# Decoder layer: the gate and up products of the first FFN unit in two halves of 256 tokens

## Chip, cores and metric

One core of a Trainium2 chip runs the whole program. The metric is device microseconds for one execution, lower is better.

## The reference

A decoder layer over 4 sequences of 512 tokens and width 512, in float32, with three stages; each ends in a layer norm (the first and second called x1 and x2 here). Cut to what matters:

```python
x1 = layernorm(x + attention(x))               # K and V with rotation, A = sum over tokens of cos(K) * cos(V)
q  = fp8(x1 * 448 / max|x1|);  c = fp8(ctx * 448 / max|ctx|)     # one scale for the whole tensor
x2 = layernorm(x1 + x1 + (q @ c) * unscale + mask)
mlp = silu(x2 @ gate_w) * (x2 @ up_w) @ down_w                   # 512 -> 2048 -> 512
out = layernorm(x2 + x2_mlp_and_experts)       # plus 8 of 1024 experts per token, chosen by two key tables
```

## The kernel before

The program is written by hand for five engines: each has its own queue, which runs in order, and waits for counts of semaphores. Tokens lie in tiles of 128 (16 tiles; four make a sequence), and the four sequences are called 0 to 3. All large matrices are multiplied in float32r with each operand split into a high part and the rest (w_hi, w_lo, x2_hi, x2_lo), so a product of the FFN is three: hi*hi, lo*hi, hi*lo. One product has 128x128 stationary values and 512 moving columns, the tokens of a sequence. The FFN weights are cut into 8 groups of 256 columns; a unit is one group for one sequence, so there are 32 units, 0 to 3 for group 0. In a unit, gate_up (L1918) makes for each of two blocks of 128 columns (c = 0 and 1) a gate product into bank gu[2c] and an up product into gu[2c+1], 12 matrix products each; down (L1951) or down_early (L1969) multiplies the result with the down weights into the four banks ob.

The change lies where the first program block (attention, x1) ends and the second begins, at 210 us, and in unit 0. What happens there before:

- The largest |x1| of all tokens is only known at the block's end, so the rounding of x1 to fp8 can start only now. For each tile ScalarE scales (L1439) and takes a rounded magnitude (L1441), both in `scaled`; VectorE adds and subtracts it (L1580, L1582, here called raise and lower), in `quantise`. TensorE multiplies with the rounded context in `cross` (L1915). The x1 of the later sequences comes to ScalarE by TensorE's transposes (L1907), through banks gu.
- VectorE adds the product to x1 (L1605, `first_residual`) and gives the negative mean (L1607). ScalarE squares the difference and sums it (L1454, `deviation`). VectorE gives the variance for two tiles (L1612), GpSimd takes the power -1/2 (L1327, `power_pair`), VectorE normalises (L1616). Then TensorE transposes x2 (L1898), ScalarE copies it as x2_hi (L1447), VectorE subtracts for x2_lo (L1627). All of this is done for the four tiles, step by step: all four rounded, then all four residuals, and so on.
- While TensorE has nothing to do, `keep_running` (L2015) lets it transpose the identity.
- The first gate products (L1933) wait for x2_hi of all four tiles, then those with x2_lo (L1936) for all four of x2_lo; the up products follow (L1888 to L1890), then `cross` of sequence 1, transposes of x1 of sequence 2, the products of c = 1 and down_early.
- The weights of group 0's down matrix are loaded at the start of the second block into w_stage[0]; ScalarE makes their high part behind x2_hi, VectorE their low part behind the first product silu(gate)*up.
- GpSimd issues the DMA that adds the mask to x1 of a sequence (L149, `add_mask`) once its x1 is transposed; at the start of the block that of sequence 1 stands ahead of both powers, later add_mask(n+2) ahead of power(n+1).
- Behind unit 0 sequence 1 has its own residuals, normalisation and transposes, which sequence 1's unit needs.

## Time and profile before

| | |
|---|---|
| median of 3 runs | 790.26 us (789.82 to 790.3) |
| the profiled execution, its own time | 789.89 us |
| span of its instructions | 788.1 us |
| TensorE busy | 770.3 us (98%) |
| VectorE busy | 665.8 us (84%) |
| ScalarE busy | 321.5 us (41%) |
| GpSimd busy | 369.1 us (47%) |

The profile names TensorE's products PE and its loads of stationary values PEld, VectorE DVE, ScalarE ACT, GpSimd POOL. Products overlap: each is shown with a duration of 0.39 us, but the next starts 0.23 us behind it, so rates are read from starts. A duration is one execution's. Idle time in brackets stands before an instruction with the engine that ended it.

### The profile page before, as it was taken

What the parts mean: (1) busy time and instruction counts of PE and PEld (TensorE: products, weight loads), DVE (VectorE), ACT (ScalarE), POOL (GpSimd) and SP (SyncE); (2) the same over time, 40 slices, a digit from 0 to 9 for tenths busy, and PEclk for the clock granted to TensorE, in tenths of its full rate; (3) what the DMA queues carried; (4) which work ended last, traced back from release to release, by engine and by line L of the source; (5) the groups of instructions that cost most, each with busy time, mean ns of one, the idle gap of its engine ahead of it and who ended that gap; (6) DMA issues with size and microseconds to landing.
All of it is one profiled execution on the core that took longest, in us unless ns stands there. A gap on an engine that the chain in (4) does not pass through costs nothing.

```text
span 788.1 us, 10623 instructions
## 1 busy us (share of the span) xinstructions
PE 770.3 (98%) x3550; PEld 631.3 (80%) x3550; DVE 665.8 (84%) x1351; ACT 321.5 (41%) x700; POOL 369.1 (47%) x323
## 2 busy tenths in 40 slices
PE   8999998999899999999999999999999999999997
PEld 6888887878667778888888888888888888888885
DVE  6889789998898870476789998999999999899876
ACT  6454346455574422222443433334333343344324
POOL 1242331432122411014466676776776677676324
PEclk9999999999999999999999999999999999999999
DMA  8666513715465638001122221431333223242014
GB/s 323 241 129 166 93 55 85 190 21 86 73 146 117 150 89 286 1 0 33 61 70 78 82 88 41 128 95 47 90 110 111 90 79 115 62 128 61 17 54 160
DMA packets 51190, 79.78 MB, mean 101 GB/s; under 512 B 17503, under 2 KB 26335, under 8 KB 50624
## 3 DMA queue, kind: packets, MB, share of 16 engines
q0 software_dynamic: 24240, 31.52, 19.0%
q1 hardware_dynamic: 25312, 47.59, 17.2%
q8 instruction: 28, 0.46, 0.2%
q10 hardware_dynamic: 1584, 0.01, 0.1%
q14 instruction: 26, 0.21, 0.1%
HBM read 110.50 MB, written 12.58 MB: 156 GB/s over the span
## 4 chain that ended last, share of the span: by engine, by line
PE 64%; DVE 4%; issue 2%; POOL 2%; ACT 1%; POOLq 0%; ACTq 0%; DVEq 0%
PE gu L1888 14%; PE gu L1889 14%; PE gu L1890 14%; PE ob L1962 7%; PE ob L1961 7%; PE ob L1966 7%; DVE scratch L1580 1%; DVE scratch L1582 1%; POOL h_lo L1316 1%; DVE x_lo L1627 1%; PE gu L2060 0%; PE ob L1915 0%; ACT junk L1454 0%; DVE xall L1621 0%; PE ob L1982 0%
## 5 line engine op out<-in xcount | busy, mean ns | idle before, releaser
L1888 PE MATMUL gu<-x_hi,w_hi 128*128 128x512 f32 x516 | 201.4, 390 | 0.0
L1890 PE MATMUL gu<-x_hi,w_lo 128*128 128x512 f32 x516 | 200.8, 389 | 0.0
L1889 PE MATMUL gu<-x_lo,w_hi 128*128 128x512 f32 x516 | 200.8, 389 | 0.0
L1316 POOL TENSOR_TENSOR h_lo<-mid,h_hi 128x512 fp32r<-128x512 f32 x62 | 87.0, 1421 | 175.8 <-ACT h_hi L1466 175.8
L1890 PEld LDWEIGHTS gu<-x_hi,w_lo 128*128 128x128 f32 x516 | 96.9, 188 | 20.2
L1888 PEld LDWEIGHTS gu<-x_hi,w_hi 128*128 128x128 f32 x516 | 96.9, 188 | 20.0
L1889 PEld LDWEIGHTS gu<-x_lo,w_hi 128*128 128x128 f32 x516 | 96.9, 188 | 19.9
L1476 ACT ACTIVATE gates<-dots 128x1 f32<-128x1 f32 x144 | 29.1, 202 | 175.2 <-DVE dots L1729 175.2
L1638 DVE TENSOR_TENSOR mid<-gu,mid 128x512 f32<-128x512 f32 x64 | 43.9, 686 | 64.1 <-PE gu L1890 54.2
L1961 PE MATMUL ob<-w_hi,h_hi 128*128 128x512 f32 x224 | 87.1, 389 | 0.0
L1962 PE MATMUL ob<-w_lo,h_hi 128*128 128x512 f32 x224 | 87.1, 389 | 0.0
L1335 POOL DMA_INDIRECT ctx_q<-table_dram,row_i x64 | 73.5, 1149 | 18.8 <-issue 17.0
L1335 POOL DMA_INDIRECT scratch<-table_dram,row_i x64 | 73.0, 1141 | 16.5 <-issue 15.1
L1466 ACT ACTIVATE h_hi<-mid 128x512 fp32r<-128x512 f32 x62 | 36.2, 625 | 85.3 <-PE ob L1966 62.2
L1966 PE MATMUL ob<-w_hi,h_lo 128*128 128x512 f32 x224 | 68.9, 389 | 0.0
L1460 ACT ACTIVATE mid<-gu 128x512 f32<-128x512 f32 x64 | 37.8, 590 | 58.9 <-PE gu L1890 50.3
L1801 DVE TENSOR_TENSOR xall<-ob,xall 128x512 f32<-128x512 f32 x93 | 58.7, 683 | 3.6 <-PE ob L1966 1.6
L1311 POOL TENSOR_TENSOR w_lo<-xhat,w_hi 128x1024 fp32r<-128x1024 f32 x21 | 50.4, 2400 | 24.1 <-ACT w_hi L1430 15.9
L1729 DVE CUSTOM_DVE_ANT_0 junk<-x_tok,ctx_q 128x512 bf16<-128x512 f32 x64 | 60.4, 944 | 0.5
L1738 DVE SCALAR_TENSOR_TENSOR xall<-ctx_q,coef,xall 128x512 f32<-128x512 f32 x64 | 60.1, 939 | 0.0
L1738 DVE SCALAR_TENSOR_TENSOR xall<-scratch,coef,xall 128x512 f32<-128x512 f32 x64 | 59.5, 930 | 0.0
L1729 DVE CUSTOM_DVE_ANT_0 junk<-x_tok,scratch 128x512 bf16<-128x512 f32 x64 | 57.1, 892 | 0.3
(254 smaller groups left out, 1431.9 us busy)
## 6 DMA issues: line engine op xcount, KB each, us to landing
stage<-in_ctx SPq DMA_DIRECT2D x7, 1024.0 KB, 6.8
total<-prod POOLq DMA_DIRECT2D x11, 384.0 KB, 4.1
xall<-half_bo POOLq DMA_DIRECT2D x4, 1024.0 KB, 9.6
xhat<-in_L_ffn_gate_w SPq DMA_DIRECT2D x8, 512.0 KB, 3.4
xhat<-in_L_ffn_up_w SPq DMA_DIRECT2D x8, 512.0 KB, 3.4
xall<-in_mask_Bx1xS_ff POOLq DMA_DIRECT2D x4, 1024.0 KB, 11.0
xhat<-in_L_ffn_down_w SPq DMA_DIRECT2D x8, 512.0 KB, 3.6
x_dram<-xall SPq DMA_DIRECT2D x4, 1024.0 KB, 7.0
```

Source lines behind the costliest of these rows:

```text
L1311: nc.gpsimd.tensor_tensor(flat(lo, r), stage_of(r, slot), flat(hi, r).bitcast(F32), ALU.subtract).then_inc(wlo_done, 1)
L1316: nc.gpsimd.tensor_tensor(lo[:, c], mid[c][:], hi[:, c].bitcast(F32), ALU.subtract).then_inc(hlo_done, 1)
L1335: nc.gpsimd.indirect_dma_start(rows[k], None, table_dram[:, :], bass.IndirectOffsetOnAxis(ap=row_i[t % 2][:, k:k + 1], axis=0), bounds_che ...
L1729: nc.vector.tensor_tensor_reduce(out=junk2[:], in0=x2_tok[par][:], in1=row[:, 0:D], scale=1.0, scalar=0.0, op0=ALU.mult, op1=ALU.add, accu ...
L1738: nc.vector.scalar_tensor_tensor(tile(t), row[:, D:2 * D], coef[:, t % 2, k:k + 1], tile(t), ALU.mult, ALU.add).then_inc(pick_done, 1)
L1801: nc.vector.tensor_tensor(tile(j), ob[i][:], tile(j), ALU.add).then_inc(acc_done, 1)
L1888: nc.tensor.matmul(dst, lhs[0], rhs[0], start=start, stop=False)
L1889: nc.tensor.matmul(dst, lhs[0], rhs[1], start=False, stop=False)
L1890: return nc.tensor.matmul(dst, lhs[1], rhs[0], start=False, stop=stop)
L1961: nc.tensor.matmul(ob[i][:], h[0][:, c, ts], w_high[:, c], start=(c == 0), stop=False)
L1962: nc.tensor.matmul(ob[i][:], h[0][:, c, ts], w_low[:, c], start=False, stop=False)
L1966: last = nc.tensor.matmul(ob[i][:], h[1][:, c, ts], w_high[:, c], start=False, stop=(c == GC - 1))
```

## The change

On TensorE, the gate and up products of unit 0 are cut in halves of 256 tokens (tiles 0 and 1, tiles 2 and 3) by two new functions, each for one bank. `high_half` makes the 8 products with x2_hi (both parts of the weights), `low_half` the 4 with x2_lo. The other products of x1 and x2 are put in between.

```diff
+                def high_half(half, c, r):
+                    pe.wait_ge(wlo_done, r + 1)
+                    pe.wait_ge(h2_done, TB // 2 * (half + 1))
+                    if half == 0:
+                        pe.wait_ge(y_scaled, TB + 2 * c + r + 1)
+                    w, cols, fs = (gate_s, up_s)[r][0], half_cols(half), slice(c * P, (c + 1) * P)
+                    for k in range(KC):
+                        for h in range(2):
+                            nc.tensor.matmul(gu[2 * c + r][:, cols], w[h][:, k, fs], x2_hi[:, k, cols], start=(half == 0 and k == 0 and h == 0), stop=False, skip_group_check=True)
+
+                def low_half(half, c, r):
+                    pe.wait_ge(l2_done, TB // 2 * (half + 1))
...
+                    for k in range(KC):
+                        last = nc.tensor.matmul(gu[2 * c + r][:, cols], w[0][:, k, fs], x2_lo[:, k, cols], start=False, stop=(half == 1 and k == KC - 1), skip_group_check=True)
+                    if half:
+                        last.then_inc((gate_mm, up_mm)[r], 1)
...
-                for i in range(TB):
+                for i in range(2):
                     transposes(1, (i,), own_bank, x1t_mm, freed(y_done, 0))
                     cross(0, nothing, (i,))
-                pe.wait_ge(y_done, TB + 2)
-                for i in range(1, TB):
+                transposes(1, (2, 3), own_bank, x1t_mm, freed(y_done, 0))
+                for i in range(2):
                     pe.wait_ge(minus_first, i + 1)
-                    keep_running(gu[0], 7)
-                pe.wait_ge(v3_ready, 2)
-                keep_running(gu[0], 4)
-                x2_transposes(0, nothing)
-                keep_running(gu[0], 3)
-                for n in range(TB - 1):
-                    gate_up(n, 0, n, 0, 2 if n == 0 else None)
-                    cross(n + 1, freed(acc_done, TB * (n - 1)) if n else nothing)
+                    keep_running(ob[3], 6)
+                cross(0, nothing, (2,))
+                x2_transposes(0, nothing, (0, 1))
+                cross(0, nothing, (3,))
+                for r in range(2):
+                    high_half(0, 0, r)
+                for r in range(2):
+                    low_half(0, 0, r)
+                high_half(0, 1, 0)
+                x2_transposes(0, nothing, (2, 3))
+                high_half(0, 1, 1)
+                for r in range(2):
+                    low_half(0, 1, r)
+                for r in range(2):
+                    high_half(1, 0, r)
+                for r in range(2):
+                    low_half(1, 0, r)
+                cross(1, nothing)
+                transposes(2, (0, 1), x1_bank(2), x1t_mm, first_half_free(0))
+                high_half(1, 1, 0)
+                low_half(1, 1, 0)
+                transposes(2, (2, 3), x1_bank(2), x1t_mm, freed(y_done, TB * 2 - 2))
+                high_half(1, 1, 1)
+                low_half(1, 1, 1)
+                down_early(0, 0, freed(z2_done, 0))
```

TensorE, from the transposes of x1 of the last tile (before) or the last two (after) to the first gate product (L2015 and L2065 are fillers, L1907 and L1939 transposes of x1 of sequence 1, L1915 and L1947 cross products of sequence 0, L1898 and L1930 transposes of x2). Before:

```order
L1907 MATMUL gu<-ident,xall 128x128 x4
L1915 MATMUL ob<-ctx_q,scratch 128x512 x4
L2015 MATMUL gu<-ident 128x128 x25
L1898 MATMUL ob<-ident,xall 128x128 x16
L2015 MATMUL gu<-ident 128x128 x3
L1933 MATMUL gu<-x_hi,w_hi 128x512
```

After:

```order
L1939 MATMUL gu<-ident,xall 128x128 x8
L2065 MATMUL ob<-ident 128x128 x12
L1947 MATMUL ob<-ctx_q,scratch 128x512 x4
L1930 MATMUL ob<-ident,xall 128x128 x8
L1947 MATMUL ob<-ctx_q,scratch 128x512 x4
L1991 MATMUL gu<-x_hi,w_hi 128x256
```

The first product of gate now follows the transposes of two tiles of x2 and the cross product of tile 3; the other two tiles are transposed further on, between products.

On VectorE, rounding, residuals, normalisation and x2_lo are cut in the same way, and the low part of the down weights (w_lo<-xhat) moves to the front. Before, at the end of the rounding (the first row is the lower of tile 2, the next two raise and lower tile 3):

```order
L1582 SCALAR_TENSOR_TENSOR scratch<-x_tok,scratch 128x512
L1580 SCALAR_TENSOR_TENSOR scratch<-x_tok,scratch 128x512
L1582 SCALAR_TENSOR_TENSOR scratch<-x_tok,scratch 128x512
L1605 SCALAR_TENSOR_TENSOR xall,z_sum<-ob,unscale,xall 128x512
L1607 TENSOR_SCALAR z_minus<-z_sum 128x1
```

After, from the second block's first row:

```order
L1655 TENSOR_TENSOR w_lo<-xhat,w_hi 128x2x512
L1597 SCALAR_TENSOR_TENSOR scratch<-scratch 128x512
L1601 SCALAR_TENSOR_TENSOR scratch<-scratch 128x512
L1597 SCALAR_TENSOR_TENSOR scratch<-scratch 128x512
L1601 SCALAR_TENSOR_TENSOR scratch<-scratch 128x512
L1775 TENSOR_TENSOR unscale<-scale_x,scale_c 128x1
L1777 TENSOR_SCALAR unscale<-unscale 128x1
L1628 SCALAR_TENSOR_TENSOR xall,z_sum<-ob,unscale,xall 128x512
L1630 TENSOR_SCALAR z_minus<-z_sum 128x1
```

The first residual (L1628, before L1605) now stands behind the rounding of two tiles, not of four. Its rest, from VectorE's part of the diff:

```diff
+                first_low_w(2, 2, 0)
+                quantise(0, (0, 1))
...
-                quantise(0, range(TB))
-                for i in range(TB):
-                    first_residual(i)
+                first_residual(0)
+                first_residual(1)
+                quantise(0, (2,))
                 first_variance(0)
+                raised = raise_y(0, 3)
+                first_normalise(0)
+                first_normalise(1)
+                lower_y(3, raised)
+                first_residual(2)
+                first_residual(3)
+                low_x2(0, (0, 1))
                 first_variance(1)
-                for i in range(TB):
-                    first_normalise(i)
-                low_x2(0)
-                quantise(1, range(TB))
+                quantise(1, (0,))
+                first_normalise(2)
+                first_normalise(3)
+                quantise(1, (1,))
+                low_x2(0, (2, 3))
+                quantise(1, (2, 3))
                 for n in range(TB - 1):
                     middle(n, 0)
-                    if n == 0:
-                        first_low_w(2, 2, 0)
```

ScalarE follows the same order, and the down weights are loaded and their high part is made in the first block already, behind the centring of the first tile of sequence 3:

```diff
+                sp.wait_ge(wlo_done, 1)
+                sp.dma_start(w_stage[0].rearrange("p (c n) -> p c n", c=GC), down_v[:, 0]).then_inc(w_in_s[0], 16)
...
                 for i in range(TB - 1):
                     centre_x1(LAST, i)
                     if i:
                         scale_x1(LAST, i - 1)
+                    else:
+                        high_down()
...
                 scaled(0, range(TB))
-                scaled(1, (0, 1))
-                for i in range(TB):
-                    deviation(i)
+                deviation(0)
+                deviation(1)
+                for i in range(3):
+                    scale_y(1, i)
+                magnitude(1, 0)
+                high_x2(0, (0, 1))
+                deviation(2)
+                deviation(3)
+                scale_y(1, 3)
+                for i in range(1, TB):
+                    magnitude(1, i)
+                high_x2(0, (2, 3))
```

GpSimd, from the second block's start (rstd is the power, L149 the DMA that adds a mask, h_lo the low part of the unit's result). Before:

```order
L1344 MEMSET key_sb 128x256
L149 DMA xall<-in_mask_Bx1xS_ff 128x4x512
L1327 TENSOR_TENSOR rstd<-var,neg_half 128x2 x2
L1316 TENSOR_TENSOR h_lo<-mid,h_hi 128x512
L149 DMA xall<-in_mask_Bx1xS_ff 128x4x512
L1322 TENSOR_TENSOR rstd<-var,neg_half 128x4
```

After:

```order
L1352 MEMSET key_sb 128x256
L1335 TENSOR_TENSOR rstd<-var,neg_half 128x2
L149 DMA xall<-in_mask_Bx1xS_ff 128x4x512
L1335 TENSOR_TENSOR rstd<-var,neg_half 128x2
L1324 TENSOR_TENSOR h_lo<-mid,h_hi 128x512
L1330 TENSOR_TENSOR rstd<-var,neg_half 128x4
L149 DMA xall<-in_mask_Bx1xS_ff 128x4x512
```

The mask of a sequence now goes out behind the power of the one before it.

## Rows read from the trace of the kernel before

**Rows 1.** List of cores: core, span, mean granted clock of TensorE.

```profile
core 0: 788.1 us, clock 0.999
```

**Rows 2.** What TensorE waited for, 225 to 788 us: total, times, longest.

```profile
PE gu L1933 <- issue: 0.4, 1, 0.4
```

**Rows 3.** Timeline of TensorE: start, us, engine, line, operation, count.

```profile
213.10 1.04 PE L1915 MATMUL ob<-ctx_q,scratch 128*128 128x512 bf16 x4 [0.86 <-DVE scratch L1582]
213.97 0.60 PE L1907 MATMUL gu<-ident,xall 128*128 128x128 f32 x4
214.43 1.04 PE L1915 MATMUL ob<-ctx_q,scratch 128*128 128x512 bf16 x4
...
222.20 2.21 PE L1898 MATMUL ob<-ident,xall 128*128 128x128 f32 x16
...
225.18 0.47 PE L1933 MATMUL gu<-x_hi,w_hi 128*128 128x512 f32 x1 [0.44 <-issue]
...
228.03 0.39 PE L1888 MATMUL gu<-x_hi,w_hi 128*128 128x512 f32 x1
...
230.75 3.63 PE L1915 MATMUL ob<-ctx_q,scratch 128*128 128x512 bf16 x16
...
241.47 0.39 PE L1978 MATMUL ob<-w_hi,h_hi 128*128 128x512 f32 x1
```

**Rows 4.** Timeline of ScalarE, same columns; idle time before it in brackets.

```profile
201.03 0.72 ACT L506 ACTIVATE xall<-xall,minus_m 128x512 f32<-128x512 f32 x1 [1.01 <-POOL minus_m L363]
...
211.43 0.67 ACT L1439 ACTIVATE scratch<-gu,scale_x 128x512 f32<-128x512 f32 x1
...
212.67 0.67 ACT L1439 ACTIVATE scratch<-gu,scale_x 128x512 f32<-128x512 f32 x1
...
214.61 0.63 ACT L1441 ACTIVATE x_tok<-scratch 128x512 bf16<-128x512 f32 x1
...
217.92 0.72 ACT L1454 ACTIVATE junk<-xall,z_minus 128x512 bf16<-128x512 f32 x1 [0.20 <-DVE z_minus L1607]
...
222.85 2.23 ACT L1447 ACTIVATE x_hi<-ob 128x512 fp32r<-128x512 f32 x4 [1.40 <-PE ob L1898]
```

**Rows 5.** Timeline of VectorE, same columns.

```profile
193.52 2.35 DVE L742 TENSOR_TENSOR w_lo<-xhat,w_hi 128x1024 fp32r<-128x1024 f32 x2
...
211.63 0.69 DVE L1580 SCALAR_TENSOR_TENSOR scratch<-scratch 128x512 f32<-128x512 bf16 x1 [1.08 <-ACT scratch L1441]
212.35 0.69 DVE L1582 SCALAR_TENSOR_TENSOR scratch<-scratch 128x512 bf16<-128x512 bf16 x1
212.96 0.68 DVE L1580 SCALAR_TENSOR_TENSOR scratch<-scratch 128x512 f32<-128x512 bf16 x1
...
216.94 0.74 DVE L1605 SCALAR_TENSOR_TENSOR xall<-ob,unscale,xall 128x512 f32<-128x512 f32 x1
...
217.82 0.75 DVE L1605 SCALAR_TENSOR_TENSOR xall<-ob,unscale,xall 128x512 f32<-128x512 f32 x1
...
221.49 0.17 DVE L1612 TENSOR_SCALAR var<-z_square 128x2 f32<-128x2 f32 x1 [0.90 <-ACT junk L1454]
221.56 2.14 DVE L1616 TENSOR_SCALAR xall<-xall,z_minus,rstd 128x512 f32<-128x512 f32 x4
223.62 2.48 DVE L1627 TENSOR_TENSOR x_lo<-ob,x_hi 128x512 fp32r<-128x512 f32 x4
```

**Rows 6.** Timeline of GpSimd, same columns.

```profile
221.74 0.93 POOL L1327 TENSOR_TENSOR rstd<-var,neg_half 128x2 f32<-128x2 f32 x1 [0.33 <-DVE var L1612]
```

**Rows 7.** Routing products (L2060): duration min/median/max, first and last start.

```profile
L2060 PEld LDWEIGHTS gu<-key_sb,ctx_q x32: 187/192/192, 315.9 to 319.5; 128*128 128x128 f32 x32
L2060 PE MATMUL gu<-key_sb,ctx_q x32: 270/275/276, 316.2 to 319.6; 128*128 128x128 f32 x32
```

**Rows 8.** Busy time of each engine, 217.95 to 222.20 us, with TensorE's clock.

```profile
217.95:222.20 4.25, 3.29 (x26) 2.70 (x26) 3.25 (x13) 3.23 (x8) 2.11 (x3) 1.00 0.66 99
```

**Rows 9.** Page, part 6: DMA issues, KB each, us to landing.

```profile
x_dram<-xall SPq DMA_DIRECT2D x4, 1024.0 KB, 7.0
```

More of the change, by code:

```diff
@@ L1235, in _ @@
                         sp.dma_start(key_sb[half * DQ:(half + 1) * DQ, s, half], keys[s]).then_inc(key_in, 16)
-                load(2, 0, 2)
                 load(3, 0, 3)
@@ L1349, in _ @@
                     low_h(n, 0)
+                    if n + 1 < TB:
+                        power(n + 1)
                     if n + 2 < TB:
                         add_mask(n + 2)
-                    if n + 1 < TB:
-                        power(n + 1)
                     low_h(n, 1)
@@ L1430, in high_w, with scale_y, magnitude, high_x2 @@
                     nc.scalar.activation(flat(hi, r), stage_of(r, slot), ACT.Copy).then_inc(whi_done, 1)
+                def scale_y(b, i):
+                    j = TB * b + i
+                    act.wait_ge(x1t_mm, j + 1)
+                    if j >= TB:
+                        act.wait_ge(q_done, j - TB + 1)
+                    nc.scalar.activation(y_q[i], gu[x1t_bank(b, i)][:], ACT.Copy, scale=scale_x[:, 0:1]).then_inc(y_scaled, 1)
+                def magnitude(b, i):
+                    act.wait_ge(y_scaled, TB * b + i + 1)
+                    nc.scalar.activation(m_q[i], y_q[i], ACT.Abs, scale=ROUND_TO_4_BITS).then_inc(y_done, 1)
                 def scaled(b, tiles):
                     for i in tiles:
-                        j = TB * b + i
-                        act.wait_ge(x1t_mm, j + 1)
-                        if j >= TB:
-                            act.wait_ge(q_done, j - TB + 1)
-                        nc.scalar.activation(y_q[i], gu[x1t_bank(b, i)][:], ACT.Copy, scale=scale_x[:, 0:1]).then_inc(y_scaled, 1)
-                        act.wait_ge(y_scaled, j + 1)
-                        nc.scalar.activation(m_q[i], y_q[i], ACT.Abs, scale=ROUND_TO_4_BITS).then_inc(y_done, 1)
-                def high_x2(b):
-                    for i in range(TB):
+                        scale_y(b, i)
+                        magnitude(b, i)
+                def high_x2(b, tiles=range(TB)):
+                    for i in tiles:
                         j = TB * b + i
@@ L1570, in _, with raise_y, lower_y @@
                 own.base, own.n = 0, first_steps[0]
+                def raise_y(b, i):
+                    dve.wait_ge(y_done, TB * b + i + 1)
+                    if b and i == 0:
+                        dve.wait_ge(cross_mm, TB * b)
+                    return own.did(nc.vector.scalar_tensor_tensor(y_q[i], m_q[i], ROUND_SUBNORMAL, y_q[i], ALU.max, ALU.add))
+                def lower_y(i, raised):
+                    own.wait(raised)
+                    nc.vector.scalar_tensor_tensor(x_q[:, i].rearrange("p c n -> p (c n)"), m_q[i], ROUND_SUBNORMAL, y_q[i], ALU.max, ALU.subtract).then_inc(q_done, 1)
                 def quantise(b, tiles):
                     for i in tiles:
[L1574 to L1582 removed]
+                        lower_y(i, raise_y(b, i))
                 def residual(b, tiles):
@@ L1621, in normalise, with low_x2 @@
                         nc.vector.tensor_scalar(tile(TB * b + i), tile(TB * b + i), mv2[:, i, 0:1], rstd2[:, i:i + 1], ALU.subtract, ALU.mult).then_inc(x2_done, 1)
-                def low_x2(b):
-                    for i in range(TB):
+                def low_x2(b, tiles=range(TB)):
+                    for i in tiles:
                         j = TB * b + i
@@ L1890, in three, with x2_transposes @@
                     return nc.tensor.matmul(dst, lhs[1], rhs[0], start=False, stop=stop)
-                def x2_transposes(b, free):
-                    for i in range(TB):
+                def x2_transposes(b, free, tiles=range(TB)):
+                    for i in tiles:
                         free(i)
```

36 lines of the change are left out of this document (17 added, 19 removed).

## The prediction

> **What bounds the kernel now.** I read four views in this order. The list of cores gives the span and the clock: 788.1 us at a granted clock of 0.999 [rows 1], the higher level (2.4 GHz) throughout. The list of what TensorE waited for, from 225 us to the end, has one line: 0.4 us before the first gate product of FFN unit 0 [rows 2]. So from 225.18 us on TensorE sets the time, and whatever moves its stream there moves the end. The same holds behind unit 2: nothing there runs by a clock of its own (the stores of x2, the table copy and the routing all start from TensorE's or VectorE's results), and it shifts as a whole.
>
> The timelines of the four engines show the stretch before that, 210 to 225 us. There TensorE does only 16 transposes of x1, 16 products of the cross attention, 16 transposes of x2 and filler transposes [rows 3]. The end of the stretch is set by a chain over all four tiles in turn: ScalarE scales x1, VectorE rounds (raise, lower), TensorE multiplies, VectorE adds the residual, ScalarE squares, GpSimd takes the power, VectorE normalises, TensorE transposes, ScalarE copies x2_hi [rows 3 to 6]. The change shortens the chain to the first product by asking for two tiles instead of four. It pays on TensorE with twice as many products of half the width.
>
> **Start of the first product.** Steps read off the rows: a raise is followed by its lower 0.72 us later and that by the next raise 0.61 later, 1.33 a tile [rows 5]. The two raises and lowers of tiles 0 and 1 start at 211.63 as before and leave VectorE free at 214.29. The low part of the down weights now stands ahead of them (two such parts took 2.35, so 1.2 [rows 5]); VectorE waits for the first magnitude until 211.63 [rows 5], so it costs 0, and without that idle time 1.2. The two small operations on unscale, 0.17 each like the variance [rows 5], come next, about 0.36 with their wait. Residual 0 starts at 214.65 instead of 216.94; its product has been ready since 214.14 (213.10 plus 1.04 [rows 3]). Residual 1 follows 0.88 later (216.94 to 217.82) at 215.53, the raise and lower of tile 2 at 216.41 and 217.13, the variance at 217.74. The two squares begin 0.98 behind their residual (217.92 against 216.94 [rows 4, 5]) at 215.63 and take 0.89 each (four between 217.92 and 221.49), so they are ready at 217.41. From a variance to the normalisation that needs it are 0.25 to GpSimd's start and 0.93 of power [rows 5, 6], 1.20 in all: 218.94. GpSimd is free for it because the power now stands ahead of the mask. The normalisations start 0.53 apart (four in 2.14), the lower of tile 3 follows at 220.00, and its product 0.75 behind (212.35 to 213.10 [rows 3, 5]) at 220.75. The transposes of tiles 0 and 1 start 0.64 behind their normalisation (221.56 to 222.20) and are over by 220.6. The product of tile 3 holds TensorE 0.87 us (213.10 to 213.97 [rows 3]), and x2_hi of both tiles is ready before that ends (0.65 behind the transposes, 222.20 to 222.85 [rows 3, 4]). **First gate product: 221.62 instead of 225.18, minus 3.56 us.**
>
> **What is given back.** (a) The products with x2_lo wait for VectorE: residual 3 needs the last cross product (220.75 plus 1.04, some 221.87), 0.88 later come two low parts at 0.61 each (four in 2.48 [rows 5]), ready at 224.05. TensorE has 16 half-width products until then, to 223.54: **plus 0.51**. (b) The transposes of tiles 2 and 3 used to lie ahead of the stream and are now in it. Four transposes take 0.46 (213.97 to 214.43 [rows 3]), two tiles 0.92, with the change of kind taken as **1.0**. They don't wait: the second variance goes out at 223.97, the power comes back at 225.17, VectorE is in a raise and lower until 225.37, the transposes can go at 226.0, and TensorE gets there at 224.05 plus 16 products, 225.97. (c) The width, 96 half products for 48 whole ones. A whole one takes 0.2267 (12 between 228.03 and 230.75 [rows 3]), 10.88 in all. The trace has no product of 256 columns. Below, half of 0.2267 is 0.1133, since the same columns must pass. Above, the routing products have 128 columns with the same size of weights and start every 0.110 (31 intervals between 316.2 and 319.6 [rows 7]), and the straight line from 128 columns at 0.110 to 512 at 0.2267 gives 0.149 at 256. I take 0.12, near the lower end: the 0.110 at a quarter of the columns looks like a floor that the load of the weights sets, the columns need 0.1133, and if the two overlap as they do at 512 the larger counts, with a little for two limits that meet. 96 times 0.12 is 11.52, **plus 0.64**. (d) A new wait: the transposes of x1 of sequence 2 into banks 0 and 1 need the magnitudes of their first two tiles. Behind the first transpose ScalarE needs 0.65 to start, 1.24 for a tile (211.43 to 212.67), 0.70 and 0.63 for the second's scale and magnitude (214.61 is 0.70 behind 211.43 plus two tiles [rows 4]), 3.22. TensorE used to fill this with 12 whole products; it now has 12 halves (1.44) and three times 0.46, 2.82: **plus 0.40**. Behind it on TensorE stands everything else.
>
> **Edits at nothing.** The high part of the down weights moves to ScalarE at 200.0, where it sat idle for 1.01 us ahead of 201.03 [rows 4]; the operation is as long as that gap. Its data is asked for when the first low part is done, about 194.7 [rows 5], beside a mask transfer. 1024 KB by the same queue landed in 7.0 [rows 9], so 512 KB should land before 201; later, it would push the last maxima of x1 one for one. GpSimd's mask for sequence 1 goes out behind the first power, at some 219.9; what needs it, the first residual of sequence 1, comes behind a product that starts at 231.8 (rival B), so it has 13 us, where a store of the same 1024 KB took 7.0 [rows 9]. The store of x2 of sequence 0 goes out with the last normalisation of that sequence, some 3 us later, and its first reader stands behind the first down products, beyond 240. Filler transposes stand only where TensorE waits.
>
> **The sum** is minus 3.56 plus 0.51, 1.0, 0.64 and 0.40: **minus 1.0 us**. The profiled execution took 789.89 (1.8 outside the span), which gives 788.9; the median of the runs is 790.26, 0.37 above it, and I carry that over: 789.3.
>
> **A rule of the skill.** The routing rows say that a load of 128 columns of weights can start every 0.110 us and hides beside a product [rows 7]. The Trainium skill (TensorE: Matmul & The Clock Gate, LDWEIGHTS) gives the load 128/1.2, 107 ns, however few columns are multiplied, and its section Back-to-back issue gap gives N/2.4 + 2.5, 109 ns at 256 columns. By these two the halves would cost 96 times 0.109 and the change would bring 1.7 us instead of 1.0. The same formula gives 216 ns for 512 columns where the rows show 227, so I don't follow it to the end.
>
> **The rivals.** **A, the narrow product is dear.** At 0.149 the 96 products cost 2.8 more than at 0.12; 0.46 of it falls into wait (a) and 0.35 into wait (d), 2.0 remain, and the change is 1.0 slower than before: 791.2. It decides at 0.135. For it speaks that the load of weights, which 512 columns hid, has no room left; against it that loads of 187 to 192 ns each still start every 0.110, so they overlap [rows 7]. **B, the next chain takes the gain.** The cross products of sequence 1 now start at 221.62 + 0.51 + 1.0 + 72 x 0.12 = 231.8, 1.0 later than before (230.75), because half 0 of both column blocks stands ahead of them. What follows, residuals to x2 of sequence 1 and the products of h on TensorE, is then no earlier. Against it: VectorE no longer has the 1.2 us of down weights in that chain and GpSimd's power no longer stands behind the mask. If it still binds, about 0.2 is left: 790.1. **C, the clock falls.** TensorE's busy share in the emptiest part, 217.95 to 222.20, is 3.29 of 4.25 at clock 1.00 [rows 8]; between 217.5 and 221.6 it would be 2.66 of 4.1. If the chip granted 1.2 GHz there, each of the half products after it would take twice as long: 48 of them cost 5.8, 795. No row shows the clock falling in a comparable gap. **D, the columns alone count.** At 0.109 to 0.113 a product, with waits as worked out, the change brings 1.4 to 1.7: 788.6. **E, the change doesn't do what it says:** the first product starts no earlier because the masks or the power of the first pair are late. The order of GpSimd's work excludes it as far as the rows go; I count it with B.
>
> **How the numbers follow.** Forecast 0.54, A 0.18, B and E 0.14, D 0.07, C or a product above 0.16 us 0.07. The likeliest is 789.3. A measurement of this kernel tells apart about 0.2%, 1.6 us. Faster than that is below 788.7: D and the lower part of the forecast (both waits gone, 0.9 more), 0.07 plus 0.11. Slower is above 791.8: C with its neighbours, and the upper part of A, 0.07 plus 0.08. Within: 0.67. The range 788.4 to 791.6 takes in D and A with 0.4 for the medians.
>
> **What would show it.** In the profile after: the first product of 256 columns at 221.6; the spacing of these products (0.12, not 0.149); a wait of 0.5 for x_lo behind 16 of them; one of 0.4 ahead of the transposes of x1 of sequence 2; the first product of down at 240.5 instead of 241.47 [rows 3]; the clock at 1.00. A start later than 223, a spacing of 0.135 or more, or an idle TensorE ahead of the x2 transposes of sequence 1 would make the prediction wrong.

## The result: 2.6 us slower

| | before | after |
|---|---|---|
| median of 7 runs each | 790.08 us | 792.66 us |
| lowest to highest | 789.82 to 790.3 | 791.41 to 793.35 |
| ratio | | 1.0029, 95% interval 1.002 to 1.0038 |
| span of the profiled execution | 788.1 us | 790.2 us |
| its granted clock | 0.999 | 0.997 |

The forecast was 789.3 with a range up to 791.6. The time lies outside it, and its sign was wrong.

The list of waits of TensorE, from 203 us on, shows the new kernel (engine and line that waited, what ended the wait, us in total, times, longest):

```profile
PE ob L1095 <- DVE xall L711: 1.7, 1, 1.7
PE ob L1947 <- DVE scratch L1601: 1.2, 2, 1.0
PE ob L1095 <- DVE amax_x L724: 1.2, 1, 1.2
...
PE ob L1930 <- DVE xall L1639: 0.8, 1, 0.8
...
PE gu L1939 <- ACT scratch L1449: 0.4, 1, 0.4
PE gu L1997 <- DVE x_lo L1650: 0.3, 1, 0.3
PE ob L2032 <- POOL h_lo L1324: 0.2, 1, 0.2
```

The last three lines are in the stream of unit 0, and two of them are the waits (d) and (a) of the prediction: 0.38 and 0.33 us, forecast as 0.40 and 0.51. They are not where 2.6 us went. The first and the third line are: TensorE's fillers at the end of the first block wait 1.7 us for an addition of VectorE (L711) that stands behind a late maximum of x1, and 1.2 us for the last maxima (L724). Before, the first of these waits did not show at all and the second was 0.4. So the loss lies ahead of everything that the sum spoke of.

ScalarE's timeline of the new kernel has its cause (start, duration, engine, line, operation; in brackets the idle time before it and what ended it):

```profile
200.06 0.72 ACT L508 ACTIVATE xall<-xall,minus_m 128x512 f32<-128x512 f32 x1 [3.61 <-POOL minus_m L365]
204.97 1.06 ACT L540 ACTIVATE w_hi<-xhat 128x1024 fp32r<-128x1024 f32 x1 [4.18 <-DMA xhat<-in_L_ffn_down_w]
205.93 0.70 ACT L508 ACTIVATE xall<-xall,minus_m 128x512 f32<-128x512 f32 x1
...
213.59 0.69 ACT L1445 ACTIVATE scratch<-gu,scale_x 128x512 f32<-128x512 f32 x1 [1.96 <-PEq L160]
```

The high part of the down weights (L540) was to fill a gap of 1.01 us [rows 4]. ScalarE instead stands still for 4.18 us in front of it, because the weights have not landed, and its queue runs in order: the centring of the next tile (L508), whose mean GpSimd had ready at 201.8, starts at 205.93 (before at 201.03 [rows 4]). The page of DMA issues for 193 to 208 us says how long the data took (KB, us from issue to landing):

```profile
xall<-in_mask_Bx1xS_ff POOLq DMA_DIRECT2D x1, 1024.0 KB, 11.3
xhat<-in_L_ffn_down_w SPq DMA_DIRECT2D x1, 512.0 KB, 9.4
```

The load was issued at 195.5 and landed at 204.9, some 0.5 us ahead of the mask for sequence 0, which GpSimd had issued at 194.1. VectorE feels it next, then TensorE:

```profile
206.67 0.69 DVE L724 TENSOR_REDUCE amax_x<-xall 128x1 f32<-128x512 f32 x1 [2.96 <-ACT xall L508]
```

The second block starts, by ScalarE's first scaling (L1445 above), at 213.59 where before's L1439 started at 210.17: plus 3.42 us.

Of these 3.42, 0.77 were there before the load was asked for. The two low parts that stood at 193.52 before [rows 5] stand at 194.29 now:

```profile
194.29 2.35 DVE L751 TENSOR_TENSOR w_lo<-xhat,w_hi 128x1024 fp32r<-128x1024 f32 x2
```

The change touches nothing ahead of them, and run 8, which differs from the changed kernel only by fillers further on, starts them at 193.43. The busy times of the engines in 124 to 130 us (TensorE's granted clock is the third figure from the end, ahead of the DMA share and GB/s), before and then after, show that this execution ran for a moment at half clock:

```profile
124.00:130.00 6.00, 5.30 (x27) 4.50 (x28) 5.83 (x11) 4.58 (x10) 1.89 (x3) 1.00 0.37 68
```

```profile
124.00:130.00 6.00, 4.66 (x14) 3.60 (x15) 5.79 (x13) 3.21 (x8) 1.91 (x3) 0.72 0.36 66
```

The dip is no work of the change: of the eleven profiled executions of this study, six had it (a clock of 0.72 over these 6 us), the one of the fastest kernel among them, and five did not. Its size varies: the other five with a dip start the low parts at 193.46 to 194.05. So I measure the load's cost from the low parts (start of w_lo) to the start of the second block:

| profiled execution | w_lo | second block | between |
|---|---|---|---|
| before | 193.52 | 210.17 | 16.65 |
| after | 194.29 | 213.59 | 19.30 |
| run 8 (after with more fillers) | 193.43 | 213.35 | 19.92 |
| run 3 (before with the early load) | 193.54 | 214.85 | 21.31 |
| run 1 (load back) | 194.05 | 210.63 | 16.58 |
| run 2 (high part last) | 193.81 | 210.41 | 16.60 |

The load costs 2.65 us in the profiled execution of the change and 3.27 in run 8's, where no dip delayed what stands ahead of it. Run 8 asks for the load 0.87 us earlier (194.67 for 195.54) but starts the high part only 0.24 earlier (204.73 for 204.97), so a late start hides some of the wait. The 4.66 of run 3 contain more than the load (see there).

From the block's start on, the change does what the sum said. TensorE's timeline after:

```profile
224.98 0.36 PE L1991 MATMUL gu<-x_hi,w_hi 128*128 128x256 f32 x1
225.18 0.28 PE L1991 MATMUL gu<-x_hi,w_lo 128*128 128x256 f32 x1
225.30 0.28 PE L1991 MATMUL gu<-x_hi,w_hi 128*128 128x256 f32 x1
...
226.86 0.28 PE L1991 MATMUL gu<-x_hi,w_lo 128*128 128x256 f32 x1
227.46 1.22 PE L1997 MATMUL gu<-x_lo,w_hi 128*128 128x256 f32 x8 [0.33 <-DVE x_lo L1650]
...
241.89 0.66 PE L1939 MATMUL gu<-ident,xall 128*128 128x128 f32 x4 [0.38 <-ACT scratch L1449]
...
243.81 0.40 PE L2028 MATMUL ob<-w_hi,h_hi 128*128 128x512 f32 x1
```

The first product of 256 columns starts 224.98 minus 213.59, 11.39 us behind the block's start; before, the first gate product came 225.18 minus 210.17, 15.01 behind it: minus 3.62, forecast minus 3.56. The narrow products start every 0.12 us (14 intervals between 225.18 and 226.86). The first product of down comes 30.22 us behind the block's start instead of 31.30: minus 1.08, forecast minus 1.0. At the first product of unit 1 it is minus 0.95 (37.95 for 38.90). In the profiled execution the sum is 0.77 plus 2.65 minus 1.08, 2.34 us at the first product of down (241.47 [rows 3] to 243.81) and 2.1 at the end. With run 8's cost of the load and the gain of the change it is 3.27 minus 0.95, 2.3 us, for 2.6 between the medians.

### The profile page after: what moved, and what is told of

The parts are those of the page before. It is cut to its first block, busy times and chain, and to the rows that moved or that the text cites. A ratio compares the mean times of both kernels' runs of the same rounds, so it can differ in the third digit from the quotient of the medians.

```text
span 790.2 us, 10688 instructions
## 1 busy us (share of the span) xinstructions
PE 770.9 (98%) x3578; PEld 635.0 (80%) x3582; DVE 666.1 (84%) x1351; ACT 321.1 (41%) x700; POOL 367.9 (47%) x323
## 4 chain that ended last, share of the span: by engine, by line
PE 69%; DVE 2%; POOL 1%; issue 1%; ACT 0%; POOLq 0%; ACTq 0%; DVEq 0%
PE gu L1920 14%; PE gu L1922 14%; PE gu L1921 14%; PE ob L2012 6%; PE ob L2016 6%; PE ob L2011 6%; PE ob L1947 1%; PE ob L2032 1%; PE ob L2028 1%; PE ob L2029 1%; PE gu L1991 0%; PE gu L1962 0%; PE gu L2132 0%; PE gu L1930 0%; PE gu L1997 0%
## 5 line engine op out<-in xcount | busy, mean ns | idle before, releaser
L1920 PE MATMUL gu<-x_hi,w_hi 128*128 128x512 f32 x504 | 196.7, 390 | 0.0
L1922 PE MATMUL gu<-x_hi,w_lo 128*128 128x512 f32 x504 | 196.3, 389 | 0.0
L1921 PE MATMUL gu<-x_lo,w_hi 128*128 128x512 f32 x504 | 196.3, 389 | 0.0
L1922 PEld LDWEIGHTS gu<-x_hi,w_lo 128*128 128x128 f32 x504 | 94.7, 188 | 19.7
L1920 PEld LDWEIGHTS gu<-x_hi,w_hi 128*128 128x128 f32 x504 | 94.7, 188 | 19.5
L1921 PEld LDWEIGHTS gu<-x_lo,w_hi 128*128 128x128 f32 x504 | 94.7, 188 | 19.5
```

The costliest lines, as they stand in the source:

```text
L1920: nc.tensor.matmul(dst, lhs[0], rhs[0], start=start, stop=False)
L1921: nc.tensor.matmul(dst, lhs[0], rhs[1], start=False, stop=False)
L1922: return nc.tensor.matmul(dst, lhs[1], rhs[0], start=False, stop=stop)
```

## The experiments

The theory: the narrow products and the new order bring about 1 us; the load that is asked for beside a mask transfer lands late and holds ScalarE's queue. The rivals: the halves don't bring what the sum says (A), the order of the work around them is what matters, or the clock does it (C). Ratios are to before's kernel on the same chip, whose median was 790.05 for the first four runs, 790.03 for the next four and 789.92 for the last.

**1. The down weights back in the second block.** The load, its high part and its low part stand where they stood before; all else is the changed kernel.

```diff
-                sp.wait_ge(wlo_done, 1)
-                sp.dma_start(w_stage[0].rearrange("p (c n) -> p c n", c=GC), down_v[:, 0]).then_inc(w_in_s[0], 16)
...
-                    else:
-                        high_down()
...
+                load(2, 0, 2)
                 load(3, 0, 3)
...
+                        high_w(2, 0, 0, 2, 0)
...
-                first_low_w(2, 2, 0)
...
+                    if n == 0:
+                        first_low_w(2, 2, 0)
```

> The kernel after with one part undone: the down weights of group 0 are loaded, and their high and low part made, in the second block again, as before the change; halves and order stay. Theory (the early load lands late and holds ScalarE in the first block): the block ends at 210.2 us again, the first half product comes at 221.6, and the 3.4 us are gone. VectorE has the low part (1.1 us) ahead of the residuals of sequence 1 again, so TensorE should idle about 1.3 us for h_lo where it idled 0.2: 790.0 to 790.4, against 790.1 before and 792.7 after. Rival (the halves and the new order cost the time themselves, in a part of the stream that the chain doesn't show): 792 or more, with the block's end at 210.2.

Measured: 789.83 us, ratio 0.9996 (0.9987 to 1.0005). Of the twelve executions eleven took 789.48 to 790.18 and one 1578.34, which is not in the ratio and for which no trace has a cause. The whole loss is gone with this edit, 2.8 us, and what remains is not to be told from before. The first product of down starts at 240.85, 30.22 us behind the block's start at 210.63. TensorE's timeline shows what then eats the gain:

```profile
247.18 0.50 PE L2026 MATMUL ob<-w_hi,h_lo 128*128 128x512 f32 x1 [0.90 <-POOL h_lo L1316]
```

The first product of unit 1 starts at 249.58, 38.95 us behind the block's start, where before's 249.07 was 38.90 behind it: the 1.08 us gained up to the down products are gone again. The wait is 0.90 where 1.3 was expected, and so the time is a little below the 790.0 to 790.4.

**2. The same load, its high part last.** ScalarE makes the high part as its last work of the first block, behind the last maxima; the load stays early.

```diff
                         scale_x1(LAST, i - 1)
-                    else:
-                        high_down()
                 for i in LAST_MAXIMA[2:]:
                     scale_x1(LAST, i)
+                high_down()
```

> The kernel after with one instruction moved: ScalarE makes the high part of the down weights as its last work in the first block, behind the scalings of sequence 3, and not behind the first centring. The load is issued where it was. Theory: the load has landed by then (at 205), nothing waits for it, the block ends at 210.2, the first half product comes at 221.6, the first down product at 240.4: 789.0 (1.1 below before), 3.5 below after. Rival (the early load itself slows the first block, by its traffic beside the mask or by SyncE's wait): the block ends later than 211 all the same, and the time stays above 791.

Measured: 788.88 us, ratio 0.9987 (0.9978 to 0.9996). Nine of the eleven executions took 788.42 to 789.05, two 790.13 and 790.2. ScalarE's timeline and the DMA issues:

```profile
201.33 0.73 ACT L508 ACTIVATE xall<-xall,minus_m 128x512 f32<-128x512 f32 x1 [1.01 <-POOL minus_m L365]
...
208.36 1.04 ACT L540 ACTIVATE w_hi<-xhat 128x1024 fp32r<-128x1024 f32 x1
```

```profile
xhat<-in_L_ffn_down_w SPq DMA_DIRECT2D x1, 512.0 KB, 9.9
```

The load is as slow as in the changed kernel, but nobody waits for it: the gap of 1.01 us is back and the high part starts without idle time. So it is the place in the queue that costs, not the traffic. Against run 1 it gains another 0.95 us, since the low part of the down weights (1.22 us of VectorE) no longer stands in the chain of sequence 1: the product silu(gate)*up of column block 1 starts 32.36 us behind the block's start instead of 33.36, the wait for h_lo falls from 0.90 to 0.20, and the transposes of x2 of sequence 1 take 0.3 less.

**3. The kernel before, with the down weights early alone.** Load, high part and low part as in the change, nothing of the halves or the new order (the edit is the reverse of that of run 1).

> The kernel before with only the edits on the down weights: early load, high part behind the first centring of sequence 3, low part first in VectorE's second block. No halves, no new order. Theory: the cost stands alone: ScalarE idles about 4.2 us ahead of the high part, the block ends at 213.6, 3.4 later than before, and nothing is given back: 793.5. Rival (the cost comes from the halves): 790, as before.

Measured: 794.57 us (793.28 to 794.9), ratio 1.0054 (1.0041 to 1.0067), 4.5 us slower than before. ScalarE's timeline:

```profile
204.88 1.06 ACT L540 ACTIVATE w_hi<-xhat 128x1024 fp32r<-128x1024 f32 x1 [4.84 <-DMA xhat<-in_L_ffn_down_w]
```

The loss comes without the halves, so they are not its cause. It is larger than the 3.4 that I expected, and the clock shows why. The busy times of the engines in two stretches (TensorE's granted clock again third from the end):

```profile
205.00:208.50 3.50, 1.12 (x10) 0.88 (x9) 1.89 (x3) 3.38 (x5) 0.00 (x0) 0.97 0.00 0
208.50:215.00 6.50, 5.44 (x23) 4.31 (x21) 3.61 (x14) 1.49 (x3) 0.82 (x2) 0.50 0.00 0
```

TensorE, idle for 2.38 us ahead of 207.91, runs at half clock from 208.5 to 215, and the fillers take nearly twice as long: 6 of them 1.54 us (at 210.16) where 6 take 0.87 in the change (at 210.25). The load landed as in run 8 (the high part starts at 204.88 and 204.73), and from the low parts to the second block this kernel needs 21.31 us where run 8 needs 19.92. So some 1.4 us are the clock's and 3.3 the load's.

**4. The mask last.** In the changed kernel GpSimd adds the mask for sequence 0 at the end of the first block instead of behind the last z of sequence 3's attention.

```diff
                 last_z_rstd(slice(0, TB))
-                add_mask(0)
...
                     last_z_rstd(slice(i, i + 1))
+                add_mask(0)
```

> The kernel after, with GpSimd's mask for sequence 0 issued as the last thing of the first block and not ahead of the last means, so that the load of the down weights has the DMA engines to itself. Theory (the load is slow since it shares the engines with the mask): it lands in 3.4 to 4 us where it took 9.4, and ScalarE waits less than 0.3 us for it. The mask then lands late, and the first residual waits for it, so the whole is no faster. Rival (the load is slow for another reason, its place in SyncE's queue or the first touch of the weights): it still takes 9 us with the mask gone.

Measured: 798.04 us, one execution. The time is spoilt by the edit itself, for the block's end now waits for the mask, and TensorE idles 9.28 us ahead of the second block. What the run was for is in ScalarE's timeline and the DMA issues:

```profile
199.47 0.72 ACT L508 ACTIVATE xall<-xall,minus_m 128x512 f32<-128x512 f32 x1 [3.60 <-POOL minus_m L365]
200.10 1.04 ACT L540 ACTIVATE w_hi<-xhat 128x1024 fp32r<-128x1024 f32 x1
```

```profile
xall<-in_mask_Bx1xS_ff POOLq DMA_DIRECT2D x1, 1024.0 KB, 10.9
xhat<-in_L_ffn_down_w SPq DMA_DIRECT2D x1, 512.0 KB, 3.2
```

Without the mask beside it the same load lands in 3.2 us instead of 9.4, and the high part starts at 200.10 without waiting, where the prediction had put it. The load is slow because of the mask. The mask itself takes 10.9 us here and in run 1 and 11.2 in before, without the load, and 11.3 to 12.0 in the eight kernels with the load beside it: it loses at most about 1 us where the load loses 6 to 7.

**5. The transposes of x1 of sequence 2 later.** Run 2, and those of tiles 2 and 3 stand behind the 8 products with x2_hi of the last up half.

```diff
-                transposes(2, (2, 3), x1_bank(2), x1t_mm, freed(y_done, TB * 2 - 2))
                 high_half(1, 1, 1)
+                transposes(2, (2, 3), x1_bank(2), x1t_mm, freed(y_done, TB * 2 - 2))
```

> The changed kernel with two edits: the high part of the down weights is ScalarE's last work of the first block (as in the run with the down weights at the tail, median 788.88), and the transposes of x1 of tiles 2 and 3 of sequence 2 stand behind the 8 products of x2_hi of the last up half instead of ahead of them. My theory: they waited 0.38 us there for a magnitude; behind 8 products (0.96 us) the magnitude is ready, ScalarE still ends its scaling before the result of column block 1 is ready for it (it waited 1.85 us there), so the wait of 0.38 goes and the time falls by 0.4 to 788.5. Rival: the later transposes push ScalarE's h_hi of column block 1 and the wait for h_lo (0.20) grows by as much: 788.9.

Measured: 788.75 us (788.36 to 789.08), ratio 0.9984 (0.9975 to 0.9993): the same as run 2. My theory fell and so did the rival's reason. The wait of 0.38 is gone and the first product of down starts at 239.91 instead of 240.64, but TensorE's list of waits has a longer one behind it, and VectorE's timelines of run 2 and run 5 say where it comes from:

```profile
PE ob L2031 <- POOL h_lo L1323: 0.8, 1, 0.8
```

```profile
240.80 2.04 DVE L1643 TENSOR_SCALAR xall<-xall,mv,rstd 128x512 f32<-128x512 f32 x4 [0.18 <-POOL rstd L1329]
242.77 0.68 DVE L1660 TENSOR_TENSOR mid<-gu,mid 128x512 f32<-128x512 f32 x1
```

```profile
240.67 2.05 DVE L1643 TENSOR_SCALAR xall<-xall,mv,rstd 128x512 f32<-128x512 f32 x4 [0.18 <-POOL rstd L1329]
242.64 0.68 DVE L1660 TENSOR_TENSOR mid<-gu,mid 128x512 f32<-128x512 f32 x1
```

The product silu(gate)*up of column block 1 (mid, L1660) stands in VectorE's queue behind the four normalisations of sequence 1 (L1643), and those hang on the cross products of sequence 1. It starts 32.36 us behind the block's start in run 2 (210.41) and 32.35 in run 5 (210.29), however early TensorE has finished the up product. From it come h_hi and h_lo. This is rival B in another place: the next chain takes the gain.

**6. Whole products.** Run 2 without the halves, in the new order.

```diff
-                for r in range(2):
-                    high_half(0, 0, r)
...
-                low_half(1, 1, 1)
+                x2_transposes(0, nothing, (2, 3))
+                pe.wait_ge(y_scaled, TB + 4)
+                gate_up(0, 0, 0, 0, 2)
+                cross(1, nothing)
+                transposes(2, (0, 1), x1_bank(2), x1t_mm, first_half_free(0))
+                gate_up(0, 0, 0, 1, None, lambda: transposes(2, (2, 3), x1_bank(2), x1t_mm, freed(y_done, TB * 2 - 2)))
```

> The changed kernel with the high part of the down weights at the tail of the first block (788.88) and with the halves undone: the new order on VectorE, ScalarE and GpSimd stays, but the gate and up products of unit 0 are 48 of 512 columns again, behind all four tiles of x2. Theory: the second normalisation starts at 225.5 in that order, x2_hi of tile 3 is ready near 228.0, so the first product goes from 221.8 to 228, and with before's 16.3 us from there to the first product of down that starts at 244.3 instead of 240.6: 792.6. Rival: the gain came from the order of the vector work, and the width only costs: the time then falls below 788.9, by the 0.64 us of the narrow products and the 1.0 us of the transposes in the stream, to 787.3.

Measured: 795.68 us (2 runs), ratio 1.0071 (1.0052 to 1.0089), 6.8 slower than run 2. The first product starts at 229.08 (expected 228). The new order makes tiles 2 and 3 later than before's did, so it pays only with the halves. Most of the time beyond the 792.6 that were expected is clock again:

```profile
222.00:224.00 2.00, 0.13 (x1) 0.00 (x0) 1.79 (x5) 1.59 (x5) 0.00 (x0) 1.00 1.12 185
224.00:226.00 2.00, 0.00 (x0) 0.00 (x0) 1.97 (x5) 2.00 (x4) 1.08 (x1) 0.64 1.06 170
226.00:228.00 2.00, 1.78 (x8) 1.57 (x8) 1.91 (x4) 0.70 (x2) 0.00 (x0) 0.50 0.91 210
```

TensorE waits 4.1 us, up to 226.22, for x2 of tiles 2 and 3; the clock falls within this wait, and it comes back at half clock. The first product of down starts 18.97 us behind the first gate product (248.05 minus 229.08) where before needed 16.29 [rows 3].

**7. Masks ahead of powers on GpSimd.** Run 2, GpSimd's queue in before's order.

```diff
-                power_pair(0)
                 add_mask(1)
+                power_pair(0)
...
-                    if n + 1 < TB:
-                        power(n + 1)
                     if n + 2 < TB:
                         add_mask(n + 2)
+                    if n + 1 < TB:
+                        power(n + 1)
```

> The changed kernel with the high part of the down weights at the tail of the first block (788.88) and with GpSimd's masks ahead of its powers again. Theory: the mask for sequence 1 waits for the four x1 transposes of TensorE (about 216.9) and then takes 1.42 us, so the first power starts at 218.4 to 219.0 instead of 218.15, and the first product 0.3 to 0.8 later than 221.81; the chain for tiles 2 and 3 moves with it, the wait for x_lo stays near 0.3: 789.2 to 789.7, and the wait for the x2 transposes of sequence 1 may show, because that sequence's power stands behind the mask for sequence 2 as well. Rival: the order of GpSimd is not what frees the power, and nothing moves: 788.9.

Measured: 790.03 us (789.96 to 790.43, 8 runs), ratio 1.0001 (0.9991 to 1.0011), 1.15 slower than run 2 and above the 789.2 to 789.7 that I expected. GpSimd's timeline:

```profile
216.55 1.34 POOL L149 DMA_DIRECT2D xall<-in_mask_Bx1xS_ff  x1 [6.11 <-PE gu L1938]
217.98 1.01 POOL L1334 TENSOR_TENSOR rstd<-var,neg_half 128x2 f32<-128x2 f32 x1
...
239.34 1.32 POOL L149 DMA_DIRECT2D xall<-in_mask_Bx1xS_ff  x1 [4.66 <-PE gu L1938]
240.18 1.55 POOL L1329 TENSOR_TENSOR rstd<-var,neg_half 128x4 f32<-128x4 f32 x1
```

The first mask costs nearly nothing: it is issued at 216.55, earlier than I thought, and the power starts 7.85 us behind GpSimd's first work of the block (210.13) instead of 7.75 in run 2. The second one costs: the power for sequence 1 starts 30.0 us behind the block's start (210.15) instead of 28.9 (239.36 for 210.41 in run 2), takes VectorE's normalisations and h_lo with it, and the wait for h_lo is 0.9 instead of 0.2; the x2 transposes of sequence 1 wait another 0.3. The place is the one that I named second.

**8. Twelve more fillers.** The changed kernel, with 28 filler transposes behind the last attention product instead of 16.

```diff
-                keep_running(16)
+                keep_running(28)
```

> The changed kernel with 12 more filler transposes on TensorE behind the last attention product of the first block, where it now idles for 1.73 us while ScalarE waits for the down weights; nothing else. Theory: of the 2.6 us that the changed kernel is slower, about 0.5 to 1.0 is the granted clock: about half of its executions show a mean clock of 0.992 and are 1 us longer, as the run of before's kernel with the early load showed half clock from 208.6 to 215 behind an idle 2.38 us. With the gap filled all executions stand near 0.997 and the median is 791.5. Rival: the gap has nothing to do with it, or the fillers stretch into the work behind: the median stays at 792.6, with clocks of 0.992 among them.

Measured: 792.15 us (10 runs, 791.49 to 795.2), ratio 1.0029 (1.002 to 1.0039). Seven runs lie between 791.49 and 792.34, three at 793.3 and above. The profiled one (793.36) still fell to half clock, a little later:

```profile
214.00:216.00 2.00, 1.32 (x9) 0.94 (x9) 1.83 (x3) 1.94 (x5) 0.00 (x0) 1.00 0.07 16
216.00:220.00 4.00, 3.79 (x12) 2.03 (x13) 2.58 (x8) 3.17 (x6) 0.00 (x0) 0.57 0.28 78
```

The edit did not do all that it was to do: TensorE's wait for the addition behind the late maximum is 1.1 us where it was 1.7, not gone. Up to 216 us it idles at most 1.2 us at a time, and the clock falls all the same. What the fall costs can be read: the first half product comes 13.02 us behind the block's start (226.37 minus 213.35) instead of 11.39, the first product of down 31.85 behind it (245.20) instead of 30.22, plus 1.63 both times. That is enough for the distance of 793.36 and 793.48 from the seven below, not for that of 795.2, of which no trace was kept. Whether the longest gap brings the fall about is not shown: the median is 0.5 below that of the changed kernel, but the runs overlap. What it can explain is bounded: even the best execution of the changed kernel (791.41) is 1.3 us above before's median, and the load of 3.27 less the gain of 0.95 gives 2.3 without any clock in the second block.

**9. The products with h_lo behind.** Run 5, and in the down products of unit 0 for column block 1 the product with h_lo of a tile stands behind those with h_hi of the next two.

```diff
                     for i in range(TB):
                         free(i)
...
-                        last = nc.tensor.matmul(ob[i][:], h[1][:, c, ts], w_high[:, c], start=False, stop=(c == GC - 1))
+                        if i >= behind:
+                            low(i - behind)
+                    for i in range(TB - behind, TB):
+                        low(i)
```

> The kernel with the later transposes (788.75) and one more edit: in the down products of unit 0 for column block 1 the product with h_lo of a token tile stands behind the two products with h_hi of the next two tiles instead of right behind its own, so that TensorE has 4 more products (0.91 us) before it needs h_lo. Theory: what the moved transposes saved came back as a wait for h_lo (0.8 us), because h of column block 1 is made behind the x2 of sequence 1 on VectorE and starts at the same time in both kernels; covered by other products the wait goes, the first product of unit 1 starts 0.8 earlier than 248.23, and the time is 788.0. Rival: a next link of the same chain (x2_hi and x2_lo of sequence 1, made on ScalarE and VectorE behind the transposes) then holds the first product of unit 1, and the time stays at 788.7.

Measured: 787.75 us (787.46 to 788.15), ratio 0.9973 (0.9963 to 0.9983), 1.0 below run 5 and the fastest of all. The wait for h_lo is gone, and the first product of unit 1 starts 37.05 us behind the block's start (247.13 for 210.08) instead of 37.94 (248.23 for 210.29). So the chain through VectorE's queue had taken the gain of run 5, and TensorE had other work to cover it.

## Why the prediction was wrong

The step that failed is the first of "Edits at nothing". It put the high part of the down weights into a gap of 1.01 us at 200.0, and said that "512 KB should land before 201; later, it would push the last maxima of x1 one for one". It landed at 204.9, 9.4 us after its issue. The case of "later" came, and nearly one for one: the data is 3.9 us later than 201, the last centring of the block 3.8 later than before's (207.15 for 203.35), the last maxima and the block's start 3.4. A term that stood in the sum at nothing measured 2.65 us, 3.27 in run 8. What was wrong is the size of the load's time, and that "later" got no price, no rival and no part of the range. The size came from the page's median of four stores, 1024 KB in 7.0 [rows 9]. These are 5.2 to 8.5 us one by one, and the first three ran beside a mask. The nearest rows in before's own trace were others: the mask transfer beside which the load runs takes 11.2 us, and the very same load of down weights takes 3.6 us at 213.6, when no mask is under way, and 8.7 at 267.8, beside a mask issued at 263.0 and a store. The page of DMA issues of before for 262 to 269 us:

```profile
xall<-in_mask_Bx1xS_ff POOLq DMA_DIRECT2D x1, 1024.0 KB, 10.8
x_dram<-xall SPq DMA_DIRECT2D x1, 1024.0 KB, 7.9
xhat<-in_L_ffn_down_w SPq DMA_DIRECT2D x1, 512.0 KB, 8.7
```

Run 4 measures the load without the mask, 3.2 us; beside it the load takes 9.4 to 10.2 (the change and runs 2, 3, 5, 6, 7 and 8). Runs 1 and 2 undo the step, each in another way, and both remove the loss; run 3 makes it in before's kernel and has it.

The Trainium skill (DMA: Bandwidth & Descriptors, Anatomy of one DMA) fits one DMA of GpSimd's as 2.0 us plus bytes over 436 GB/s, an estimate of 3.2 us for 512 KB: run 4, with a load of SyncE's, agrees. The same page (Queues, rings and completion order) says that each of the 16 engines takes its queues in turn, a packet at a time. By an even share the load of half the mask's bytes would have been through well before the mask; the traces show it landing only 0.2 to 0.5 us ahead of the mask's end. Why, no run here shows.

The other steps, in the order of the prediction:

- **Start of the first product**: minus 3.56 forecast, minus 3.62 measured from the block's start. Right.
- **(a) the wait for x_lo**: 0.51 forecast, 0.33 measured.
- **(b) transposes in the stream**: no wait ahead of those of tiles 2 and 3, as forecast. For the price of 1.0 see the sum.
- **(c) the width**: 0.12 us a product, as chosen; rival A (0.149) is out, and so is D (0.109 to 0.113).
- **(d) the wait for the magnitudes**: 0.40 forecast, 0.38 measured.
- **The sum** from the block's start to the first product of down: minus 1.0 forecast, minus 1.08 measured. From the first gate product to the first of down the change gives back 2.54 us (18.83 for 16.29), forecast 2.55. That this is so close is in part luck: (a) is 0.18 below its forecast, and once (a), (c) and (d) are taken off, 1.19 remain for (b) instead of 1.0. The transposes of tiles 2 and 3 hold TensorE 0.79 us (229.49 to 230.28); the rest is not split here.
- **Rival B** (the next chain takes the gain) was rejected for the wrong place. Sequence 1's x2 transposes don't wait, but h_lo does: 0.2 us in the change and 0.8 or 0.9 in runs 1, 5 and 7. In run 1, where the down weights' low part stands in that chain as before, it takes the whole gain; it is what makes run 2 faster than run 1.
- **Rival C** (the clock) did not come in the profiled execution of the change, neither in its emptiest part, 221 to 225 us, nor anywhere else from 205 to 225 (1.00). It did in run 8's, which has the same second block: 0.57 from 216 to 220, ahead of the stretch that I had looked at, for 1.63 us. The prediction priced the fall behind the first half product, at 5.8 us; here the clock is back before it. Three of the seven executions of the change have a mean clock of 0.992 and lie at 792.7 to 793.4; a fall as in run 8 or in run 3 would explain them, but none of the three has a trace. So the 0.3 us between the 2.3 that the traces give and the 2.6 of the medians stays open.

With the one edit of run 2 the change is 1.2 us faster than before, where 1.0 was forecast.

## What to carry to other kernels

An operation that is moved into an idle gap of an in-order queue has to be ready when its turn comes, and what makes it ready must be priced as carefully as the operation: read the transfers that are already in flight at its issue, not the time of a like transfer elsewhere. If the queue has a place behind everything that others wait for (run 2), it costs nothing there even though the load takes 9.9 us. And when a wait of TensorE is removed and the time doesn't move, look at the next in-order queue: put independent products in front of the one that waits (run 9).

## What the chip showed that I had not expected

- A 512 KB load issued by SyncE lands in 3.2 us without a mask transfer (run 4) and in 9.4 to 10.2 us beside a 1024 KB accumulating transfer issued by GpSimd 1.4 us earlier (seven kernels). The latter takes 10.9 to 11.2 us without the load (before, runs 1 and 4) and 11.3 to 12.0 with it.
- TensorE's clock fell to the lower of its levels behind idle times of 2.4 us (run 3, half clock for 6.5 us) and within one of 4.1 us (run 6), but also where no idle time was longer than 1.2 us (run 8, 216 to 220 us), and not in the profiled execution of the change, which idled 1.7 and 1.2 us. The length of one gap alone does not tell these cases apart.
- In six of eleven profiled executions, of faster and slower kernels alike, the clock over 124 to 130 us was 0.72. The low parts at 193.5 then start at 193.46 to 194.29 instead of 193.43 to 193.67. One execution alone can be off by 0.8 us, as much as most edits here move.
